# Macaron block on one core: the plain feed-forward splits its operands from PSUM, the last attention pair is reordered, and register waits in the attention loop are merged

## The reference

```python
x = x + 0.5 * ffn(layernorm(x))                 # ternary weights, SwiGLU and two hidden layers of 512
# the attention block, on layernorm(x):
x = x + linear_attention(layernorm(x) * g1 + b1)  # 16 heads of 64, cumulative over the sequence
h = layernorm(x) * g2 + b2
x = x + gelu(h @ Wf1) @ Wf2                      # "plain" feed-forward, 128 -> 512 -> 128
x = x + 0.5 * ffn(layernorm(x))                 # the ternary block once more
```

## Time and profile before

| | us |
|---|---|
| median of 3 executions | 859.92 |
| lowest, highest | 857.48, 861.05 |
| profiled execution, its time | 858.43 |
| profiled execution, its span | 856.6 |
| PE busy | 800.9 (93%) |
| DVE busy | 563.5 (66%) |
| ACT busy | 568.5 (66%) |
| POOL busy | 367.2 (43%) |

### The profile page before, as it was taken

One profiled execution on the slowest core, in us unless ns is written; L12 is line 12 of the kernel. 1 busy time (PEld: TensorE's weight loads), 2 busy tenths in 40 slices (PEclk: granted clock), 3 DMA queues, 4 the chain that ended last, 5 costly groups with the idle time before them and its releaser, 6 DMA issues.

```text
span 856.6 us, 28172 instructions
## 1 busy us (share of the span) xinstructions
PE 800.9 (93%) x11682; PEld 677.0 (79%) x11682; DVE 563.5 (66%) x1305; ACT 568.5 (66%) x1024; POOL 367.2 (43%) x292
## 2 busy tenths in 40 slices
PE   1799999999999999999999999999888799999997
PEld 0588878877788888888888888887776678888886
DVE  7665565366868778687778768768688682828220
ACT  3687777767655666565666565665767477777774
POOL 4597979682001001010100101001376497979784
PEclk9999999999999999999999999999999999999999
DMA  7002120201001001010100102101124310201010
GB/s 258 0 26 58 42 65 10 78 10 51 15 3 41 9 0 50 0 49 0 33 16 0 50 0 59 28 0 38 39 58 114 100 51 13 61 13 50 1 50 26
DMA packets 56700, 33.53 MB, mean 39 GB/s; under 512 B 1984, under 2 KB 55232, under 8 KB 56640
## 3 DMA queue, kind: packets, MB, share of 16 engines
q1 hardware_dynamic: 56640, 32.79, 13.2%
HBM read 22.29 MB, written 10.49 MB: 38 GB/s over the span
## 4 chain that ended last, share of the span: by engine, by line
PE 65%; ACT 13%; DVE 11%; issue 6%; POOL 4%; DMA 1%; SPq 0%; DVEq 0%; ACTq 0%; POOLq 0%
PE ps L676 33%; PE ps L836 13%; PE ps L647 6%; ACT ee L1208 4%; PE ps L884 3%; PE ps L933 3%; PE ps L915 3%; ACT rr L1209 3%; PE ps L903 3%; POOL alA L1740 1%; DVE kt L1530 1%; PE ps L739 1%; POOL alB L1740 1%; DVE am L1592 1%; ACT full L1172 1%
## 5 line engine op out<-in xcount | busy, mean ns | idle before, releaser
L1208 ACT ACTIVATE ee<-ps 128x512 f32<-128x512 f32 x128 | 78.7, 615 | 102.0 <-PE ps L836 80.0
L1842 POOL TENSOR_TENSOR as<-as,power 128x4 f32<-128x4 f32 x16 | 19.0, 1190 | 287.0 <-DVE as L1550 256.9
L1740 POOL TENSOR_TENSOR alA<-full,ahA 128x512 fp32r<-128x512 f32 x74 | 100.6, 1373 | 40.8 <-DVE ahA L1384 34.8
L676 PE MATMUL ps<-ahA,wh 128*128 128x512 f32 x288 | 113.5, 394 | 1.1 <-POOL alA L1740 1.0
L1376 DVE SCALAR_TENSOR_TENSOR full<-ps,sc,gate 128x512 f32<-128x512 f32 x64 | 46.6, 747 | 103.2 <-PE ps L676 64.4
L676 PE MATMUL ps<-ahB,wh 128*128 128x512 f32 x288 | 113.4, 394 | 0.6 <-POOL alB L1740 0.6
L676 PE MATMUL ps<-alA,wh 128*128 128x512 f32 x288 | 112.3, 390 | 0.0
L676 PE MATMUL ps<-alB,wh 128*128 128x512 f32 x288 | 112.2, 390 | 0.0
L1740 POOL TENSOR_TENSOR alB<-full,ahB 128x512 fp32r<-128x512 f32 x76 | 99.6, 1323 | 13.1 <-ACT ahB L1115 7.4
L1114 ACT ACTIVATE full<-ps,sc 128x512 f32<-128x512 f32 x86 | 59.5, 692 | 32.9 <-PE ps L676 22.8
L1209 ACT ACTIVATE rr<-ps 128x512 f32<-128x512 f32 x128 | 79.0, 617 | 0.0
(11 more groups left out here) (180 smaller groups left out, 2203.3 us busy)
## 6 DMA issues: line engine op xcount, KB each, us to landing
wst<-in_ternary SPq DMA_DIRECT2D x5, 512.0 KB, 7.8
stage<-in_attn SPq DMA_DIRECT2D x4, 512.0 KB, 4.8
xlnA<-x_scratch SPq DMA_DIRECT2D x8, 256.0 KB, 2.8
axr<-x_scratch SPq DMA_DIRECT2D x8, 256.0 KB, 3.1
yx_scratch<-ay SPq DMA_DIRECT2D x8, 256.0 KB, 2.3
xs_scratch<-axs SPq DMA_DIRECT2D x8, 256.0 KB, 2.4
xlnA<-yx_scratch SPq DMA_DIRECT2D x8, 256.0 KB, 3.2
xlnB<-yx_scratch SPq DMA_DIRECT2D x8, 256.0 KB, 3.4
```

The source lines that it names most:

```text
L676: ins = nc.tensor.matmul(b[:, :], w[:, col(k):col(k) + P], x_[:, k, :], start=(k == 0 and j == 0), stop=(k == ks[-1] and j == terms - 1))
L1208: nc.scalar.activation(ee[k][:, :], src[:, :], ACT.Exp).then_inc(*X["act"].step(f"e_{name}"))
L1740: return nc.gpsimd.tensor_tensor(dst, src, hi.bitcast(F32), ALU.subtract)
```

## The change

**Splits from PSUM.** ACT now first writes `hi`, waits for its own instruction, and then writes the full value back into the PSUM bank that it read (in place). DVE makes `lo` = bank - hi: `f_norm_low` for the normalised tile (before, POOL did that from SBUF) and `lo1`, `lo3` in `f_split`. Slices 0 and 2 stay with POOL and SBUF. A bank is now released by the DVE subtraction, no longer by ACT's last read.

**Order in the plain feed-forward.** DVE: normalise(t+2), stats(t+3), norm_low(t+1), residual(t-2), split(t). SP: `f_load(t+4)` ahead of the store and of the residual load.

**Last pair.** PE: `f_norm(0)` and `f_norm(1)` ahead of `output_projection`. DVE: `f_normalise(0)`, `(1)` at the head of the pair. ACT: table load and `f_norm(0)`, `(1)` ahead of `output_rows`.

**Loop.** `hold` takes several waits at once, leaves out one that an earlier wait of the same turn covers, and puts one always-satisfied wait ahead of a group. The two halves of `scores`, `outputs` and `state_products` now wait together, ahead of the first. The value projections move one place later among the four query projections.

The core of the diff:

```diff
-                for j, h in ((0, None), (1, 0), (2, 1), (3, None)):
+                for j, h in ((0, None), (1, None), (2, 0), (3, 1)):
...
             for k in range(2, NT):
+                if k + 4 < NT + 2:
+                    f_load(k + 4)
                 f_store(k - 2)
                 f_residual(k)
-                if k + 4 < NT + 2:
-                    f_load(k + 4)
-                else:
+                if k + 4 >= NT + 2:
...
-            def hold(sem, value, per):
-
-                if rolled:
-                    value = pe.to_reg(rolled[0] * per + (value - per))
-                    if small:
-
-                        pe.wait_ge(X["pe"].sem, X["pe"].base)
-                pe.wait_ge(sem, value)
+            def hold(*wanted, small=False):
+                ready = []
+                for sem, value, per in wanted:
+                    if rolled and seen.get(id(sem), 0) < value:
+                        seen[id(sem)] = value
+                        ready.append((sem, pe.to_reg(rolled[0] * per + (value - per))))
+                    elif not rolled:
+                        ready.append((sem, value))
+                if rolled and small and ready:
+                    pe.wait_ge(X["pe"].sem, X["pe"].base)
+                for sem, value in ready:
+                    pe.wait_ge(sem, value)
...
+                f_norm(0)
+                f_norm(1)
                 output_projection(hh - 1)
-                f_norm(0)
                 transposed_keys(o)
                 back(hh - 1)
-                f_norm(1)
...
             def f_norm(t):
                 wait(act, "pe_fn", "T", t)
-                wait(act, "pool_fn", "lo", t - 2)
-                nc.scalar.activation(f_full[t % 2], src, ACT.Identity, **gain).then_inc(*T["act_fn"].step("full"))
-
-                wait(act, "pe_f1", f"{KT - 1}", t - 2)
                 nc.scalar.activation(nh[t % 2][:, :], src, ACT.Identity, **gain).then_inc(*T["act_fn"].step("hi"))
+                wait(act, "act_fn", "hi", t)
+                nc.scalar.activation(src, src, ACT.Identity, **gain).then_inc(*T["act_fn"].step("full"))
...
+                    if m % 2:
+
+                        wait(act, "act_f1", f"hi{m}", t)
+                        nc.scalar.activation(src, src, ACT.Gelu).then_inc(*T["act_f1"].step(f"full{m}"))
...
+            def f_norm_low(t):
+                wait(dve, "act_fn", "full", t)
+
+                wait(dve, "pe_f1", f"{KT - 1}", t - 2)
+                nc.vector.tensor_tensor(nl[t % 2][:, :], f_norm_ps(t), nh[t % 2][:, :].bitcast(F32), ALU.subtract)\
+                    .then_inc(*T["dve_fn"].step("lo"))
...
                 for t in range(2, NT):
-                    if t == 2:
-                        residual(NHALF - 1)
                     f_normalise(t + 2)
-                    f_split(t)
-                    f_residual(t - 2)
                     if t + 1 < NT:
                         f_stats(t + 3)
+                        f_norm_low(t + 1)
+                    f_residual(t - 2)
+                    f_split(t)
```

More of the change, by code:

```diff
@@ L445, in attention_plan @@
                     values(turn(), o, h)
+                if last:
+                    for t in range(2):
+                        tail(turn(), f"N{t}", "dve_fn", "lo", t)
                 bank = turn()
@@ L449, in attention_plan @@
                     act.append(f"wf{hh - 1}")
-                bank = turn()
-                if last:
-                    tail(bank, "N0", "act_fn", "hi", 0)
+                if not last:
+                    turn()
                 kt((turn(), turn()), o)
@@ L797, in _, with made @@
             X = attn
-            rolled, small = [], []
-            def hold(sem, value, per):
-                if rolled:
-                    value = pe.to_reg(rolled[0] * per + (value - per))
-                    if small:
-                        pe.wait_ge(X["pe"].sem, X["pe"].base)
-                pe.wait_ge(sem, value)
+            rolled, seen = [], {}
+            def hold(*wanted, small=False):
[10 more added lines that the diff above has]
+                    pe.wait_ge(sem, value)
+            def made(steps, name):
+                return *steps.done(name, 0), sum(X["pair"][e] for e in ENG if steps is X[e])
             def after(eng, name):
-                hold(*X[eng].done(name, 0), X["pair"][eng])
+                hold(made(X[eng], name))
             def bank(name):
@@ L815, in bank @@
                     steps, by, _ = X["banks"].prior[name]
-                    hold(*steps.done(by, 0), sum(X["pair"][e] for e in ENG if steps is X[e]))
+                    hold(made(steps, by))
                 return ps[X["banks"].bank[name]]
@@ L821, in emptied @@
                 last = {}
-                for steps, by, _ in [X["banks"].prior[n] for n in names if n in X["banks"].prior] + [*more]:
-                    if type(steps) is Made:
-                        pe.wait_ge(*steps.done(by, 0))
-                    else:
-                        last[id(steps)] = max(last.get(id(steps), (0, "")), (steps.at[by], by))
-                for e in ENG:
-                    if id(X[e]) in last:
-                        after(e, last[id(X[e])][1])
+                for steps, by in [X["banks"].prior[n][:2] for n in names if n in X["banks"].prior] + [*more]:
+                    sem, value, per = made(steps, by)
+                    if last.get(id(sem), (0, 0))[1] < value:
+                        last[id(sem)] = sem, value, per
+                hold(*last.values(), small=True)
             def three(b, pairs, name):
@@ L1036, in attention_pe @@
                     rolled.append(i)
+                    seen.clear()
                     pair(1)
@@ L1665, in attention_dve @@
                     c, i, e, o, last = 2 * (hh % 2), hh // 2, 2 * hh, 2 * hh + 1, hh + 1 == NHALF
+                    if last:
+                        for t in range(2):
+                            f_normalise(t)
                     for h in range(2):
@@ L1805, in f_rstd @@
                     rstd(t % 2, PAIR[t % 2], NI)
-            def f_norm(t):
-                wait(pool, "act_fn", "hi", t)
-                rest(nl[t % 2][:, :], f_full[t % 2], nh[t % 2][:, :]).then_inc(*T["pool_fn"].step("lo"))
             def f_low(t, m):
```

130 lines of the change are left out of this document (63 added, 67 removed).

## The result

The changed kernel took 856.04 us as a median (854.77 to 856.6) and the kernel before, on the same chip, 859.98: a ratio of 0.9951 [0.9932, 0.9969], 4.2 us less by the ratio. The profiled execution took 854.77 with a span of 853.0, 3.6 less than the 856.6 of before. My forecast was 854.3 in a range of 850.3 to 857.6. The table of where the time went shows that the way to the number was not the forecast one.

What follows compares the result with a forecast made beforehand. PE carries 65% of the chain and waits in the feed-forward for DVE's 7.9 us turn. Terms -1.7 + 2.9 - 3.4 - 3.4 = -5.6 take 858.43 to 852.8; the median lies 1.5 above, 854.3, range 850.3 to 857.6.

Steps and rivals of the forecast that it cites:

- The loop of attention, 0: Attention loop: thinner and merged waits and the new query order change nothing, 0, at most 2 or 3 us over 14 turns.
- this is no register wait, and thinner waits uncover nothing: Attention loop: PE's 0.36 us "issue" idle per output, 8.0 us in all, is not register waiting, so thinner waits give 0.
- ACT does the same ten pieces in either order: Attention loop's query order: ACT's work is the same whichever order queries and values take; 0, to -0.6 us.
- The last pair, -1.7: Last attention pair to norm(3): early norm tiles remove PE's 1.88 us wait, leaving smaller ones of 0.4 and 1.0; -1.7 us.
- The entry, +2.9: norm(3) to norm(5): tile 6's statistics wait for its load and delay norm_low(4), from 1.7 ahead to 1.2 behind; +2.9 us.
- The loop, -3.4: Feed-forward, norm(5) to norm B: PE bounds at 6.6 us a tile plus 1.8 clock loss, 28.2 against 31.62; -3.4 us.
- the clock decides: Feed-forward loop: 3.7 us idle ahead of norm(5) lowers PE's clock, +1.8 on tile 4, so lo0 misses the normalisation.
- the rival's 6.95: Feed-forward loop: without clock loss POOL's lo0 collides with DVE's normalisation and DVE's turn is 6.95 us; chance 0.18.
- The end, -3.4, else -1.9: norm B to the ternary block: 4.1 us against 7.48 if PE bounds, -3.4; 5.6 if DVE bounds, -1.9.
- the rival's number and cause: norm B to the ternary block, DVE bound: residual ahead of split leaves 1.9 idle, 5.6 us, -1.9; chance 0.18.
- No cost of PSUM: ACT's writes into PSUM cost as into SBUF (0.59 to 0.60, 0.76 us); DVE's PSUM subtractions and POOL don't delay each other.
- The single-input cast, which the prediction left open: DVE's split: by the skill's rule the cast, in a two-port mode, would hold POOL; no profile row showed it apart.

Runs made afterwards that it cites:

- e3: The kernel before with only the attention loop's new waits, repeats dropped and halves merged; 851.68 us, ratio 0.9912.
- e2: The changed kernel with the old order of queries and values in the attention loop; 853.58 us, ratio 0.9920.
- e1: The changed kernel with VectorE writing lo1 of tile 1 before the low part of tile 2's normalisation; 847.42 us, ratio 0.9858.
- e5: The changed kernel with GpSimd's power ahead of its low part of piece 0 in the feed-forward loop; 855.09 us, ratio 0.9940.
- e8: The kernel before with repeated waits dropped but the two halves' waits not merged; 850.24 us, ratio 0.9880.
- e9: e7 with GpSimd's low part of the third block's first normalisation behind tile 7's last low part; 840.53 us, ratio 0.9775.
- e11: e7 with the waits of the two halves of score, output and state blocks apart again; 840.68 us, ratio 0.9775.
- e7: The changed kernel with early lo1 of tile 1, old query order, tile 6's load first and GpSimd's power first; 841.35 us, ratio 0.9776.

## Why the prediction was right in its number and wrong in its way

- **The loop of attention, 0.** Wrong: 4.76 gained, made of 7.3 by the waits (e3) and 2.6 lost by the order of queries (e2). The step that failed is "this is no register wait, and thinner waits uncover nothing". The first half was right and the second doesn't follow from it. The same for "ACT does the same ten pieces in either order": it does, but no longer has one to fill the time in which VectorE is late.
- **The last pair, -1.7.** The chain of waits that I counted was right (e1: -1.3), but the step that failed is the one from there to norm(3), which has no word of f_last(0)'s bank. Of the banks I had checked those of the key transpose and of back(14), which moved to norm tiles, and not the ones whose *reader* the split had changed. It cost 9.3 (41.13 against 31.80).
- **The entry, +2.9.** The mechanism stands, in e1: +2.3 from norm(3) to norm(5), with the load behind the store of xs; the load took 3.15 from its issue to the statistics in the changed kernel, forecast 3.5. In the changed kernel it was -0.3, since the pause of 9.37 let VectorE run ahead.
- **The loop, -3.4, "the clock decides".** Measured -4.5. The clock did not fall at norm(5), where the pause was 1.80 and not the forecast 3.7, and VectorE's collision set 6.90, the rival's 6.95. With the 3.33 of e1 the clock fell, and PE was the bound at 6.41 (forecast 6.6): -4.4. The two are as nearly equal as forecast.
- **The end, -3.4, else -1.9.** -1.99, the rival's number and cause; -3.6 in e1.
- **No cost of PSUM.** Right: 0.58 and 0.75 for ScalarE's writes back (0.60 and 0.78 for its hi parts into SBUF), 0.69 for VectorE's parts, and none of these is held up by GpSimd. The Trainium skill (SBUF — State Buffer, "Who interferes with whom") has this for VectorE instructions with at most one SBUF input, outside the two-port modes. The trace agrees: 0.68 at 652.71 in e5 with GpSimd's 1.30 from 652.65, and the normalisation, with its two SBUF inputs, at 2.85, 1.79 or 1.13 with two, one or no low part of GpSimd inside. The single-input cast, which the prediction left open, is held: 0.92 in e5, 0.42 alone.

So two errors, +9.7 in the pair and -4.8 in the loop, stand against each other, and what they leave is partly met by the feed-forward, which gave 2.9 more than forecast: -3.6 and not -5.6. That the sum came out near is luck. Without the bank the change is what e1 is, 11.8 us of span less than before.

## What to carry to other kernels

When an edit gives a buffer another last reader, list everything that waits for that buffer and ask where the new reader stands in its engine's program; a row whose releaser writes a tile that the waiting instruction doesn't read is a buffer's release. Between small pipelined instructions look from start to start, not at idle time, and drop waits that an earlier one has already covered. Where two engines lock each other out, a loop can settle in either of two rhythms, so that mending one pause can bring little until the order that keeps it in the good one is mended too.

## What the runs showed of the hardware

A wait that is already met, with the register instruction that goes with it, isn't free for TensorE's stream: 15 waits and 12 register instructions fewer in a pair took 0.7 us off every other pair (25.53 to 24.84, e8) and about half of that off the rest, with no row of idle time that shows it. Behind pauses of 0.87 (e9), 1.69 and 1.80 us (the changed kernel) and 1.88 (the kernel before, at 606.50) the granted clock stayed 1.00; behind 1.89 (e11), 1.91 (e5, e7), 3.33 (e1) and 9.37 it fell to between 0.50 and 0.65, and the twelve wide matmuls behind took 4.1 to 5.3 us and not 2.9. The length of a pause alone doesn't tell the two apart at 1.88 and 1.89; what else decides, these runs don't show. A VectorE cast with one SBUF input takes 0.92 us and not 0.42 where a GpSimd subtraction of 1.30 has begun before it (e5).
